# Bias rows and ones in tiles of 128 rows: one change to a graph-network kernel

## The reference

```python
# layer 1, its end: a norm over all nodes, then a product with a bias
h = norm_w * hc / sqrt(var + EPS) + norm_b
x = layernorm(x + h @ final_W.T + final_b)
# layer 2
agg = segment_sum(h[src] * norm[:, None], dst)   # h = x @ W, with self loops
x = layernorm(x + relu(agg + b))
# layer 3
y = segment_sum((x @ W)[edge_src] * edge_weight[:, None], edge_dst) + b
x = layernorm(x + relu(layernorm(y) * gamma + beta))
```

## Time and profile before

| | |
|---|---|
| time, median of 3 runs | 5445.98 us (5443.33 to 5457.53) |
| the profiled execution | 5451.02 us, its span 5449.3 us |
| granted clock over the span | 0.854 of 2.4 GHz |
| PE busy | 4425.4 us (81%) |
| VectorE busy | 4275.3 us (78%) |
| POOL busy | 4065.4 us (75%) |
| ScalarE busy | 3651.6 us (67%) |
| transfers | 1213.28 MB, mean 223 GB/s |

### The profile page before, as it was taken

One profiled execution on the slowest core, in us unless ns is written; L12 is line 12 of the kernel. 1 busy time (PEld: TensorE's weight loads), 2 busy tenths in 40 slices (PEclk: granted clock), 3 DMA queues, 4 the chain that ended last, 5 costly groups with the idle time before them and its releaser, 6 DMA issues. The chain is left out here.

```text
span 5449.3 us, 83007 instructions
## 1 busy us (share of the span) xinstructions
PE 4425.4 (81%) x18558; PEld 2619.7 (48%) x18558; DVE 4275.3 (78%) x8746; ACT 3651.6 (67%) x9127; POOL 4065.4 (75%) x4125
## 2 busy tenths in 40 slices
PE   6999999999999978999999999999677756661000
PEld 4555555555555433444444577777444534541000
DVE  7888888888888656878788799999788854457776
ACT  3777777777777635666666688888688854446665
POOL 6788888888888777777776277777777767777777
PEclk9999999999999989999999999999755555565555
DMA  6777787777777547777777699999789866774443
GB/s 179 208 210 203 199 208 205 200 205 206 202 203 209 149 113 209 204 208 203 205 204 206 216 363 362 364 358 369 264 284 281 278 203 227 229 236 158 135 135 104
DMA packets 850456, 1213.28 MB, mean 223 GB/s; under 512 B 347598, under 2 KB 517000, under 8 KB 850214
## 3 DMA queue, kind: packets, MB, share of 16 engines
q1 hardware_dynamic: 744566, 1059.81, 61.2%
q0 software_dynamic: 100352, 149.23, 12.6%
q10 hardware_dynamic: 5296, 1.73, 0.1%
HBM read 648.60 MB, written 438.76 MB: 200 GB/s over the span
## 5 line engine op out<-in xcount | busy, mean ns | idle before, releaser
L843 ACT ACTIVATE p_s<-p_ps,cols 128x512 f32<-128x512 f32 x588 | 404.6, 688 | 341.2 <-PE p_ps L797 216.7
L725 POOL DMA_INDIRECT home<-edge_row_cols,scatter_cols x392 | 446.2, 1138 | 119.3 <-issue 119.3
L1192 POOL DMA_INDIRECT ring_rows<-t_rows,home_cols x384 | 410.4, 1069 | 119.2 <-issue 88.5
L198 POOL DMA_INDIRECT out<-u_res,scatter_cols x392 | 407.7, 1040 | 121.7 <-issue 118.4
L191 POOL DMA_INDIRECT u_rows<-t_rows,home_cols x392 | 387.9, 990 | 145.9 <-issue 116.5
L191 POOL DMA_INDIRECT ring_rows<-t_rows,home_cols x400 | 400.3, 1001 | 126.4 <-issue 118.4
L718 POOL DMA_INDIRECT p_xs<-in_x,src_cols x388 | 387.3, 998 | 123.3 <-issue 117.0
L718 POOL DMA_INDIRECT p_xd<-in_x,dst_cols x388 | 399.1, 1028 | 107.2 <-issue 107.2
L1201 POOL DMA_INDIRECT home_cols<-home,src_cols x376 | 368.0, 979 | 142.6 <-issue 86.1
L212 DVE BATCH_NORM_STATS2 r_counts<-r_v 128x6 f32<-128x256 f32 x980 | 373.3, 422 | 10.1
L227 ACT ACTIVATE r_x<-r_v,r_nm,r_rs 128x128 f32<-128x128 f32 x784 | 321.8, 482 | 81.8 <-DVE r_nm L1768 81.8
(11 more groups left out here) (304 smaller groups left out, 14013.1 us busy)
## 6 DMA issues: line engine op xcount, KB each, us to landing
ring_rows<-in_x SPq DMA_DIRECT2D x98, 512.0 KB, 6.1
p_xT<-p_xt SPq DMA_DIRECT2D x392, 128.0 KB
t_rows<-p_o SPq DMA_DIRECT2D x98, 512.0 KB, 7.8
p_x1T<-p_oT SPq DMA_DIRECT2D x392, 128.0 KB
hT<-ring_own SPq DMA_DIRECT2D x98, 512.0 KB
q_hn<-hT SPq DMA_DIRECT2D x98, 512.0 KB
r_h<-hT SPq DMA_DIRECT2D x98, 512.0 KB
r_x<-t_rows SPq DMA_DIRECT2D x98, 512.0 KB
```

The costliest lines, as they stand in the source:

```text
L198: nc.gpsimd.indirect_dma_start(out=table, out_offset=bass.IndirectOffsetOnAxis(ap=idx[:, j:j + 1], axis=0), in_=rows[:, j, :], in_offset=N ...
L725: nc.gpsimd.indirect_dma_start(out=tab["home"], out_offset=bass.IndirectOffsetOnAxis(ap=s["scat"][:, k:k + 1], axis=0), in_=s["at"][:, k:k ...
L843: nc.scalar.activation(act_out[i][:, :], flat(bank_r if i else bank_t), ACT.Silu, bias=col(LS0 + i)).then_inc(r_act[i], 1)
L1192: nc.gpsimd.indirect_dma_start(out=rows[:, e % 4, j, :], out_offset=None, in_=tab["t1"], in_offset=bass.IndirectOffsetOnAxis(ap=s["home"][ ...
```

## The change

The tiles of the bias products get 128 rows. Rows 3 to 127 are zero, so that the sums are as before. `ones3` is cleared whole, then its rows 0 to 2 are set to one, behind a wait of POOL for its own clear. `b2x3`, `b3x3` (in `setup`) and `row3` (in `nodes23`) are cleared by POOL; code that writes or copies their rows now names rows 0 to 2. PE's first product in `nodes23` waits for three clears in place of two. VectorE's wait for the clears moves from behind `split_row` to ahead of it and asks for three.

```diff
-            ... ones3=sb("ones3", [3, P], BF16),
-            b2x3=sb("b2_x3", [3, G, H], BF16), ..., b3x3=sb("b3_x3", [3, G, H], BF16),
+            ... ones3=sb("ones3", [P, P], BF16),
+            b2x3=sb("b2_x3", [P, G, H], BF16), ..., b3x3=sb("b3_x3", [P, G, H], BF16),
@@ setup, gpsimd
-            nc.gpsimd.memset(s["ones3"][:, :], 1.0)
+            nc.gpsimd.memset(s["ones3"][:, :], 0.0).then_inc(consts, 1)
+            nc.gpsimd.memset(s["b2x3"][:, :, :], 0.0)
+            nc.gpsimd.memset(s["b3x3"][:, :, :], 0.0)
+            pool.wait_ge(consts, 7)
+            nc.gpsimd.memset(s["ones3"][0:3, :], 1.0)
@@ nodes01, sync
-                                         s["b2x3"][:, 0, :]).then_inc(b2_copied, DMA)
+                                         s["b2x3"][0:3, 0, :]).then_inc(b2_copied, DMA)
@@ nodes01, vector (bias_rows)
-                split_row(nc, s, row3[:, 0, :], first["part"], first["rest"], then)
+                split_row(nc, s, row3[0:3, 0, :], first["part"], first["rest"], then)
-                    i = nc.vector.tensor_copy(row3[:, j, :], row3[:, 0, :])
+                    i = nc.vector.tensor_copy(row3[0:3, j, :], row3[0:3, 0, :])
@@ nodes23
-        row3, zeros3 = sb("r_row3", [3, G, H], BF16), sb("r_zeros3", [3, BLK], BF16)
+        row3, zeros3 = sb("r_row3", [P, G, H], BF16), sb("r_zeros3", [P, BLK], BF16)
@@ nodes23, gpsimd
             nc.gpsimd.memset(zeros3[:, :], 0.0).then_inc(cleared, 1)
+            nc.gpsimd.memset(row3[:, :, :], 0.0).then_inc(cleared, 1)
@@ nodes23, tensor
-                    pe.wait_ge(cleared, 2)
+                    pe.wait_ge(cleared, 3)
@@ nodes23, vector
-            split_row(nc, s, row3[:, 0, :], part, rest, then)
+            dve.wait_ge(cleared, 3)
+            split_row(nc, s, row3[0:3, 0, :], part, rest, then)
-                i = nc.vector.tensor_copy(row3[:, j, :], row3[:, 0, :])
+                i = nc.vector.tensor_copy(row3[0:3, j, :], row3[0:3, 0, :])
-            dve.wait_ge(cleared, 1)
```

More of the change, by code:

```diff
@@ L284, in build @@
             b3=sb("b3_row", [P, H]), g3=sb("gamma_row", [P, H]), be3=sb("beta_row", [P, H]),
-            default=sb("default_row", [P, H]), rs3=sb("rs3_cols", [P, NB * G]), ones3=sb("ones3", [3, P], BF16),
-            b2x3=sb("b2_x3", [3, G, H], BF16), b2x36=sb("b2_x36", [9 * G, G, H], BF16), b3x3=sb("b3_x3", [3, G, H], BF16),
+            default=sb("default_row", [P, H]), rs3=sb("rs3_cols", [P, NB * G]), ones3=sb("ones3", [P, P], BF16),
+            b2x3=sb("b2_x3", [P, G, H], BF16), b2x36=sb("b2_x36", [9 * G, G, H], BF16), b3x3=sb("b3_x3", [P, G, H], BF16),
             blocks=sb("norm_block_sums", [P, 2, NB + EB]), sums=sb("norm_sums", [P, 2]),
```

## The result

The changed kernel took 5419.68 us (median of 5 runs, 5410.58 to 5421.21) against 5445.98 us. The profiled execution took 5410.58 us for a span of 5408.9 us, 40.4 us less than the profiled one of before. It is the fastest of its five, and the profiled one of before lies 5 us above its median. So the pair of traces shows 14 us more than the 26 us between the medians, and it serves here to say where the time went, not how much it was.

What follows compares the result with a forecast made beforehand. It took the DMA transfers (7.95 us a round at 363 GB/s) to bound nodes23 and POOL's gathers edges3. Ramp -4 us, steady stage, edges3 and clears 0 gave 5442 us against the 5446.0 us median; range 5420 to 5456 us.

Steps and rivals of the forecast that it cites:

- the reading of the queue: Nodes23: over 3 us of DMA work always queued, so transfers at 363 GB/s set the 7.95 us round.
- almost one number: Nodes23: PE's 7.90 us and the transfers' 7.95 us a round; the larger was read as the bound.
- the ramp: First rounds of nodes23: PE sets the pace; 21 bias products at 0.20 us save 4 us, bounds 0 and 7.
- Edges3 costed at nothing: Edges3: POOL's queue of gathers covers the shorter bias products, so they save 0 us.
- Height, not number format: PE's bias products: differing height makes two holes; closing them saves 0.20 us each, bounds 0 and 0.21.
- the steady stage at nothing: Nodes23, about 90 rounds: PE's saved 1.0 us a round becomes waiting for `r_h`; 0 us gained.
- (3): Setup and start of nodes23: POOL's added clears and moved waits are covered, 0 us; uncovered under 2 and 0.5 us.
- (4): VectorE's row work, SP's transfers and edges2's bias product stay as before: zero.
- Rival B: Nodes23: PE really set the pace, transfers can exceed 363 GB/s, VectorE's 7.72 us comes next; 5420 us, chance 0.15.
- Rival D: Nodes23: PE's waits of about 1 us a round lower its clock to mean 0.95; 5474 us, chance 0.08.
- The signs announced: Nodes23: `r_h` waits 80 us or more, PE idle about 1 us a round, ScalarE's 36.6 us transpose wait shrinking, rounds 7.95 us.
- B's sign: Nodes23: a rate of 370 GB/s or more, with VectorE near 100%, would show that PE had set the pace.

Runs made afterwards that it cites:

- deep_ring: Changed kernel with rings of nine blocks instead of six for `r_h` and `r_x`, loads issued a round earlier; 5392.39 us, 0.9884 of the kernel before.
- after_more_dma: Changed kernel with an extra load of 128 KB a round into a tile nobody reads; 5414.9 us, 0.9938 of the kernel before.
- before_loads_first: Kernel before with the store of `r_x3` moved behind the next round's four loads in SP's order; 5442.56 us, 0.9988.
- before_deep_ring: Kernel before with rings of nine blocks instead of six for `r_h` and `r_x`, loads issued a round earlier; 5447.73 us, 0.9996.
- edges3_high: Changed kernel keeping 128 rows only for edges3's bias products, the others taking rows 0 to 2; 5456.59 us, 1.0012 of the kernel before.
- height64: Changed kernel with the bias products taking rows 0 to 63 of the same cleared tiles; 5445.43 us, 0.9998 of the kernel before.
- before_no_bias: Kernel before without nodes23's bias products from the second group on; 5434.11 us, 0.9967.
- norm_high: Changed kernel keeping 128 rows only for nodes23's three norm bias products a round, others rows 0 to 2; 5421.1 us, 0.9954 of the kernel before.
- layer2_high: Changed kernel keeping 128 rows only for nodes23's two layer-2 bias products a round, others rows 0 to 2; 5424.05 us, 0.9968 of the kernel before.

## Why the prediction was wrong, point by point

The step that failed is the reading of the queue, in the first part: "A queue that always holds 3 us of work never starves", hence a mean round "as long as the transfers take". The runs show that 363 GB/s at a share of 0.99 was no limit. The same queue moved 378 GB/s in the same kernel when asked for more, 389 in `deep_ring` and 394 in `after_more_dma`. The 8 us from issue to landing said how long one load takes beside others, not that the rate was spent. That a wait for `r_h` ended last in up to 50 of 83 rounds was true, but those waits were worth 0.07 us a round, the mean above the median; with them gone (`before_loads_first`, `before_deep_ring`) the round was still 7.90 us. The forecast set "almost one number" against another, and the larger was no cause. The timeline of one round without a hole in PE was the better witness. A second term was too small: the ramp, put at 4 us, measured 9.4.

Point by point:
- Edges3 costed at nothing: right, though PE's busy time there fell by a fifth (`edges3_high`). Its transfers and gathers did not notice.
- Height, not number format: right (`height64`). The size was off: 0.30 us a product, not 0.20, as the result shows. I had taken the hole behind the bias product up to the first f32 product only. The rows to see it by were there: eight f32 products from 3503.22 to the next bias product at 3504.31 are 1.09 us, where eight equal steps of 0.11 are 0.88; 0.10 of the rest is the hole ahead and 0.11 the one I missed. With the forecast's bound it made no difference; PE's round became 6.40, not 6.90.
- The Trainium skill, on the page "TensorE: Matmul & The Clock Gate", in its Part 3, "Packing small matmuls" (The mechanism), lists weight loads as overlapping a running product only when the row groups differ. The paragraph ahead of that list names a second case, a load into the background weight buffer, which the prediction left out. This case's trace goes against the list and can't say which buffer was used: products of equal height follow at 0.11 us with their loads hidden, and where the height changes there are three holes of 0.10 us.
- (2), the steady stage at nothing: wrong, by the step above. The mean round fell by 0.29 us, which is 24.8 us over 84 rounds.
- (2), the ramp at 4 us: too small. Up to the ninth square root the changed kernel was 9.4 us quicker. The forecast reckoned 21 products at 0.20 us; at 0.30 they are 6.3 us. It also took the full clock for granted, where its own row for 3077 to 3085 us reads 0.56. In the changed kernel the clock rose 11 us sooner, and the queue's share of 0.96 in that window goes with it. How much of the 9.4 us is the clock's, no run parts. In `after_more_dma`, where the clock rose only at 3080.1 us, the ninth square root came 68.9 us behind the first clear, 1.7 us later than in the changed kernel.
- (3) and (4), the clears and waits: right, nothing, by `height64`.
- Rival B had the mechanism and the time (5420 us), the time by luck. It took VectorE's 7.72 busy us as the next floor, but 0.40 us of that was a hidden wait (last section), and the floor is the 7.43 us of ScalarE and VectorE together. The changed kernel missed this floor because the loads, issued against a ring of six, came late. Its mean of 7.68 us fell near B's 7.72 for another reason than B's.
- Rival D, the clock: PE was idle about 1.1 us a round, and the clock held at 0.99. Yet D exists in small. Four rounds of the changed kernel took 9.4 to 10.6 us. One of them:

```profile
3244.35 0.60 PE L234 MATMUL r_ps_t<-ident,r_y 128*128 128x128 f32 x4
3246.88 0.40 PE L1604 MATMUL r_ps_n<-r_row,ones 128*128 128x512 bf16 x1 [1.93 <-DMA r_h<-hT]
3247.11 1.88 PE L1606 MATMUL r_ps_n<-r_wn,r_h 128*128 128x128 f32 x8
```

```profile
3246.00:3248.00 2.00, 1.12 (x6) 1.10 (x7) 1.93 (x7) 1.84 (x11) 1.27 (x1) 0.78 0.98 344
3248.00:3250.00 2.00, 2.00 (x10) 1.85 (x10) 1.86 (x6) 1.33 (x4) 1.49 (x3) 0.50 0.99 329
3250.00:3252.00 2.00, 2.00 (x16) 1.95 (x15) 1.02 (x2) 1.49 (x9) 2.00 (x4) 0.87 1.03 419
```

  After a load that was 1.93 us late the granted clock is 0.50, that is 1.2 GHz, and the eight products take 1.88 us instead of 1.05. By the three windows (0.78, 0.50, 0.87) the low level lasted 3.4 us. It came twice more between 3140 and 3780 us, behind holes of 2.3 and 2.4 us in PE, but not behind the longest, 2.90 us, so the length of the hole alone doesn't settle it:

```profile
3678.44 0.39 PE L1604 MATMUL r_ps_n<-r_row,ones 128*128 128x512 bf16 x1 [2.90 <-DMA r_h<-hT]
3678.67 1.05 PE L1606 MATMUL r_ps_n<-r_wn,r_h 128*128 128x128 f32 x8
```

  In `before_no_bias`, where PE had least to do, the low level came twenty times in that window (mean clock 0.94). That may be part of why it is slower than the changed kernel; no run took the clock's share apart. In `deep_ring`, where PE's waits are short (at most 1.0 us), the clock is 1.00.
- The signs announced: the waits for `r_h` over 80 us, PE idle over 1 us a round, and the transposes' wait down from 36.6 to 15.2 us all came, as the forecast's signs. They came under rival B too, so they told nothing apart. The one that did was the rate: 370 GB/s or more was named as B's sign, and 377 was measured. B's other sign, VectorE near 100%, told nothing either: it was 97% busy in both kernels. The forecast's rounds of 7.95 us at 363 GB/s did not come.

Left open: why `norm_high` and `layer2_high`, with PE at 7.00 and 7.30 us, keep median rounds of 7.63 and 7.67 us where the changed kernel's is 7.43. Since SP's loads wait for PE's norm groups, a slower PE issues later loads; that is argued, not shown. And the last stage spreads by itself: from edges3's first gather to the end it is 1063.8 us in the profiled run of `deep_ring`, the slowest of its four, and 1046.0 us in that of the changed kernel, though the two do not differ there. So `deep_ring`'s 27 us between the medians, against 20.8 us in nodes23 of the traces, is known to some microseconds only.

## What to carry to other kernels

A DMA share near 1 and long landing times are no capacity: put a few per cent more bytes on the queue, or find the stretch with the highest rate, before the queue is called the bound. Read the bound from one round's timeline, where an engine without a hole is the pace, and ask of the busy time of each other engine whether a wait is hidden in it. Then work out what the next chain takes, waits included. When the pace setter gets quicker, loads that are tied to its progress have less time to land: deepen their ring in the same change.

## What was not expected of the hardware

- A product whose height differs from its neighbours' cost 0.30 us in three holes of 0.10: ahead of it, behind it, and ahead of the second product behind it. It did so at 3 rows and at 64 alike, beside 128.
- The DMA share does not measure the rate. The stage showed shares of 0.90, 0.95, 0.99, 1.01, 1.02, 1.02 and 1.03 with 333, 351, 363, 377, 378, 389 and 394 GB/s: from 0.99 up, 4% more share carried 8.5% more bytes. The 384 GB/s of one stretch of 32 us, called the exception, was below what was held over 640 us. The Trainium skill, "DMA: Bandwidth & Descriptors", section "Bandwidth", gives 425 GB/s for one core alone, measured on 16 MB from HBM. No run here shows it: over 640 us none came above 394, and over 32 us (3178 to 3210 us of `after_more_dma`) it was 410.
- A single stall of TensorE of 1.93 us was followed by 3.4 us at half the granted clock, in a stage in which it was otherwise busy 86% of the time; one of 2.90 us was not.
- A wait can be counted as busy time. The first scaling of the guard on VectorE, 128 x 20 values, stands in the groups by line (3140 to 3780 us) of the kernel before and of `deep_ring` with means of 578 and 181 ns (323 in the changed kernel):

```profile
L1793 DVE TENSOR_SCALAR r_guard<-r_counts 128x20 f32<-128x20 f32 x80 | 46.2, 578 | 2.7
```

```profile
L1800 DVE TENSOR_SCALAR r_guard<-r_counts 128x20 f32<-128x20 f32 x87 | 15.8, 181 | 3.0
```

  The next instruction, the second scaling, waits for ScalarE's squares (`squared`). One round of the kernel before, VectorE and then ScalarE:

```profile
3502.69 0.58 DVE L1793 TENSOR_SCALAR r_guard<-r_counts 128x20 f32<-128x20 f32 x1
3503.19 0.16 DVE L1797 TENSOR_SCALAR r_guard<-r_ssq 128x8 f32<-128x8 f32 x1
```

```profile
3502.87 0.19 ACT L1651 ACTIVATION_READ_ACCUMULATOR r_sq<-r_v 128x1 f32 x1
```

  The second scaling starts 0.13 us behind the end of the last square, and the first is on record as busy up to 0.08 us past that start. Both distances are the same, to some hundredths of a microsecond, in nearly all rounds of the three traces, whatever the first one's length. So 0.40 of the 0.46 us by which VectorE's round shrank was a wait for ScalarE, which itself waited 36.6 us, 0.44 us a round, for PE's transposes.
